# Attention block with an MLP: weight chunks loaded by halves, mask rows copied half as often, and small steps of the opening moved

## The reference

```python
q = _ln(queries, q_norm_g, q_norm_b); kv = _ln(tokens, kv_norm_g, kv_norm_b)
qp = q @ in_proj_w[:D].T + in_proj_b[:D]          # kp, vp from kv in the same way
scores = jnp.einsum('bhld,bhtd->bhlt', qh, kh) / np.sqrt(hd)
dist = jnp.sqrt(jnp.maximum(jnp.sum(diff * diff, axis=-1), 0.0))
scores = scores - spatial_scale * dist + spatial_offset
scores = jnp.where(key_padding, -jnp.inf, scores); attn = softmax(scores)
x = queries + (attn @ v) @ out_proj_w.T + out_proj_b
h = gelu(_ln(x, mlp_norm_g, mlp_norm_b) @ mlp_w1.T + mlp_b1)
x = x + (h @ mlp_w2.T + mlp_b2)
```

## Time and profile before

| | us |
|---|---|
| median of 3 runs | 1239.07 (1238.29 to 1239.6) |
| the profiled execution | 1240.29 |
| its span, first to last instruction | 1238.5 |
| PE busy | 1209.4 (98%) |
| POOL busy | 992.2 (80%) |
| DVE busy | 935.5 (76%) |
| ACT busy | 876.5 (71%) |

### The profile page before, as it was taken

How to read it: one execution, slowest core, us unless ns; L and a number is a source line. 1 busy time by engine, 2 the same in 40 slices (tenths; PEclk the granted TensorE clock), 3 DMA queues, 4 the chain that set the end, 5 groups by cost and what they waited for, 6 DMA issues and landing times.

```text
span 1238.5 us, 27536 instructions
## 1 busy us (share of the span) xinstructions
PE 1209.4 (98%) x9320; PEld 788.6 (64%) x9320; DVE 935.5 (76%) x2467; ACT 876.5 (71%) x2062; POOL 992.2 (80%) x1287
## 2 busy tenths in 40 slices
PE   7899899999999999999999999999999999999998
PEld 3444465666666666666666666667666666666664
DVE  5789998888877787888877787788777777677321
ACT  6889777777767776777767776777767776776331
POOL 5587999989897989989897989989898987767320
PEclk9999999999999999999999999999999999999999
DMA  8599998998998898999889998988989998888544
GB/s 240 156 204 224 251 233 183 209 209 178 208 195 212 194 224 179 213 206 184 202 192 217 196 221 183 214 201 188 203 192 209 197 216 171 168 177 176 143 113 125
DMA packets 469693, 241.69 MB, mean 195 GB/s; under 512 B 385056, under 2 KB 409904, under 8 KB 469552
## 3 DMA queue, kind: packets, MB, share of 16 engines
q1 hardware_dynamic: 469552, 239.93, 86.3%
HBM read 109.66 MB, written 12.58 MB: 99 GB/s over the span
## 4 chain that ended last, share of the span: by engine, by line
PE 85%; SPq 4%; POOL 3%; DVE 3%; issue 2%; ACT 2%; DMA 1%; POOLq 0%; DVEq 0%; ACTq 0%
PE ps_down L685 26%; PE ps_up L670 26%; PE ps_qk L605 12%; PE ps_vo L629 6%; PE ps_vo L626 6%; PE ps_s L641 4%; PE ps_pv L655 4%; SPq L401 1%; SPq L423 1%; POOL soft L1341 1%; SPq L392 1%; POOL p_nat L1333 1%; SPq L462 1%; DMA w_stage<-in_w_qkv 0%; SPq L376 0%
## 5 line engine op out<-in xcount | busy, mean ns | idle before, releaser
L670 PE MATMUL ps_up<-hT,w 128*128 128x256 f16 x3072 | 377.2, 273 | 2.0 <-ACT u L884 1.3
L685 PE MATMUL ps_down<-w,hid 128*128 128x512 f16 x1536 | 372.8, 379 | 0.5 <-DVE hid L1177 0.4
L670 PEld LDWEIGHTS ps_up<-hT,w 128*128 128x128 f16 x3072 | 300.2, 98 | 91.8 <-issue 2.4
L1333 POOL TENSOR_SCALAR p_nat<-soft,row_inv 128x256 f16<-128x256 f32 x480 | 296.1, 626 | 62.5 <-DVE row_inv L1135 60.5
L837 ACT ACTIVATE soft<-soft,neg_max 128x256 f32<-128x256 f32 x512 | 255.2, 500 | 124.1 <-DVE neg_max L1127 123.3
L1127 DVE CUSTOM_DVE_ANT_0 soft<-ps_s,soft,factor 128x256 f32<-128x256 f32 x512 | 225.6, 476 | 142.3 <-PE ps_s L641 142.1
L1145 DVE SCALAR_TENSOR_TENSOR p_nat<-soft,row_inv,p_nat 128x256 f16<-128x256 f32 x480 | 266.4, 594 | 2.1 <-POOL p_nat L1333 2.1
L1341 POOL TENSOR_SCALAR soft<-dist,scale_neg,offset 128x512 f32<-128x512 f32 x256 | 248.7, 971 | 14.1 <-DVE p_nat L1145 10.3
L884 ACT ACTIVATE u<-ps_up,bias,up_scale 128x256 f32<-128x256 f32 x256 | 142.2, 556 | 133.4 <-PE ps_up L670 133.4
L685 PEld LDWEIGHTS ps_down<-w,hid 128*128 128x128 f16 x1536 | 148.6, 97 | 132.0 <-DMA w<-x_scratch 1.1
L1349 POOL TENSOR_SCALAR hid<-u,hid_scale 128x1024 f16<-128x1024 f32 x64 | 81.3, 1271 | 102.7 <-ACT u L890 102.3
(11 more groups left out here) (135 smaller groups left out, 1568.2 us busy)
## 6 DMA issues: line engine op xcount, KB each, us to landing
w<-x_scratch SPq DMA_DIRECT2D x256, 256.0 KB, 3.1
stack<-qk_parts SPq DMA_DIRECT2D x256, 96.0 KB
raw<-in_ctx SPq DMA_DIRECT2D x32, 256.0 KB, 3.5
raw<-in_x SPq DMA_DIRECT2D x32, 256.0 KB, 3.1
c_stage<-in_w SPq DMA_DIRECT2D x32, 256.0 KB, 4.0
x<-in_x SPq DMA_DIRECT2D x32, 256.0 KB, 3.3
out<-x SPq DMA_DIRECT2D x32, 256.0 KB, 3.2
tok_rows<-in_tok_xy SPq DMA_DIRECT2D x16, 256.0 KB, 3.8
```

Source lines behind the costliest of these rows:

```text
L670: mm = e.matmul(ps_up[s % 2][:, 0:L], w_1_sb[:, wp, k, m * P:(m + 1) * P], hT[:, b % 2, :, xp * KT + k, :], start=(k, wp, xp) == (0, 0, 0) ...
L685: mm = e.matmul(ps_down[tt][:], hid[:, chunk % HID_RING, i, hp, tt * P:(tt + 1) * P], w_2_sb[:, s % W2_RING, wp, :], start=(m == 0 and (hp ...
L1333: mine = e.tensor_scalar(p_nat[:, nat, HI, lc, :], soft[:, ring, lc, :], row_inv[:, ring, lc:lc + 1], 1.0, ALU.mult, ALU.mult)
```

## The change

- W1 and W2 are loaded in 16 DMAs of 512 KB in place of 32 of 256 KB, one every second slot, each when both quarters that it overwrites have been split; each staging buffer has two semaphores instead of four.
- `stack_copies` copies the mask row only for the first two groups of a batch (each ring place once a batch), and `n_stack` counts accordingly.
- `row_q` gets its own place, so `dist_square` no longer waits for the DMA that reads it; `bias_rows_1` takes that wait over.
- `masks` moves from slot -5 to -24 (DVE), `keep_mask` from -4 to -18 (SP).
- `dist_sqrt(0)` moves from slot -4 to -6, ahead of the sum of V's squares (ACT). The squares of the first two quarters move from slots -4 and -3 to -2.
- The row of V: `weight_bias` from slot -3 to 0 (PE), `bias_row` from -2 to 1 (ACT), `bias_turn` from -1 to 2 (SP), `bias_v_spread` from 3 to 4 (DVE). `keep_busy` in slot 0 counts 16 steps more as taken (as slot 4 does), and `warm` in slot -6 has 8 matmuls instead of 6.

```diff
--- before.py
+++ after.py
@@ -153,7 +153,7 @@
         sq = sb("sq", [P, LC, T], F32, at["x1_n"])
 
         row_kv = sb("row_kv", [1, D], F32, at["x1"] + KT * D * 4)
-        row_q = sb("row_q", [1, D], F32, at["x1_n"])
+        row_q = sb("row_q", [1, D], F32, at["h_nat"] + 2 * D * 2)
         rows_1 = sb("rows_1", [P, D], F32, at["x1"] + (KT + 1) * D * 4)
         bias_v = sb("bias_v", [P, KT, P], F32, at["x1"] + KT * D * 4)
         mask_u8 = sb("mask_u8", [B, T], U8, at["x1"] + (KT + 1) * D * 4)
@@ -214,7 +214,7 @@
         s_m1, s_u, s_gelu, s_hidhi, s_hidlo, s_m2, s_out = [
             sem(n) for n in ("s_m1", "s_u", "s_gelu", "s_hidhi", "s_hidlo", "s_m2", "s_out")]
         s_w2, s_store = sems("s_w2_", W2_RING), sems("s_store", X1_RING)
-        s_w, s_wk, s_wq, s_wc = sems("s_w", 2), sems("s_wk", KT), sems("s_wq", KT), [sems(f"s_wc{i}_", KT) for i in range(C_STAGES)]
+        s_w, s_wk, s_wq, s_wc = sems("s_w", 2), sems("s_wk", KT), sems("s_wq", KT), [sems(f"s_wc{i}_", 2) for i in range(C_STAGES)]
         s_colsq, s_colsum, s_wsq, s_tot, s_mix, s_n2, s_pow, s_gs, s_cst = [
             sem(n) for n in ("s_colsq", "s_colsum", "s_wsq", "s_tot", "s_mix", "s_n2", "s_pow", "s_gs", "s_cst")]
         s_whi, s_wlo, s_w2st, s_invw, s_wh = sem("s_whi"), sem("s_wlo"), sems("s_w2st", W2_RING), sem("s_invw"), sem("s_wh")
@@ -263,7 +263,8 @@
             return 2 * G + which + 1
 
         def n_stack(G):
-            return 5 * DMA * (G // STACK_RING + 1)
+
+            return DMA * (HPG * (G // STACK_RING + 1) + G // HG + 1)
 
         def n_pt(i):
             return DMA * (i // PT_RING + 1)
@@ -352,11 +353,13 @@
             src = w_o if sec == SEC_O else w_qkv[:, sec * D:(sec + 1) * D]
             return src.rearrange("(k p) n -> p k n", p=P)
 
-        def c_src(n, k):
+        def c_half(n, half_of):
             if n < N_CHUNKS:
-                return w_1[k * P:(k + 1) * P, n * D:(n + 1) * D]
-            m = KT * (n - N_CHUNKS) + k
-            return w_2[m * P:(m + 1) * P, :]
+                rows = w_1[2 * half_of * P:(2 * half_of + 2) * P, n * D:(n + 1) * D]
+            else:
+                m = KT * (n - N_CHUNKS) + 2 * half_of
+                rows = w_2[m * P:(m + 2) * P, :]
+            return rows.rearrange("(k p) n -> p k n", p=P)
 
         def staged(n, k):
             return c_stage[n % C_STAGES][:, k, :]
@@ -390,8 +393,9 @@
                     src = qk_parts[32 * j:32 * j + 32, :, G % 2:G % 2 + 2, :].rearrange("p r w l -> p r (w l)")
                     dst = stack[0:96, ring, j, :, :].rearrange("p w l -> p (w l)")
                     e.dma_start(dst, src).then_inc(s_stack[ring], DMA)
-                src = mask_kept[b:b + 1, :].rearrange("p (o t) -> p o t", o=1).to_broadcast([1, HPG, T])
-                e.dma_start(stack[96:97, ring, :, 1 - query_side(G), :], src).then_inc(s_stack[ring], DMA)
+                if G % HG < STACK_RING:
+                    src = mask_kept[b:b + 1, :].rearrange("p (o t) -> p o t", o=1).to_broadcast([1, HPG, T])
+                    e.dma_start(stack[96:97, ring, :, 1 - query_side(G), :], src).then_inc(s_stack[ring], DMA)
 
             def p_turn(i):
                 gate.wait_ge(s_plo, i + 1)
@@ -454,12 +458,13 @@
                 for k in range(KT):
                     e.dma_start(w_stage[sec][:, k, :], w_src(sec)[:, k, :]).then_inc((s_wk if sec == SEC_K else s_wq)[k], DMA)
 
-            def load_chunk(n, k):
+            def load_chunk(n, half_of):
 
                 if n >= C_STAGES:
-                    gate.wait_ge(s_wlo, n_piece(n - C_STAGES, k))
+                    gate.wait_ge(s_wlo, n_piece(n - C_STAGES, 2 * half_of + 1))
                     gate.wait_ge(s_brow, 3 + min(n - C_STAGES + 1, N_CHUNKS))
-                e.dma_start(staged(n, k), c_src(n, k)).then_inc(s_wc[n % C_STAGES][k], DMA)
+                dst = c_stage[n % C_STAGES][:, 2 * half_of:2 * half_of + 2, :]
+                e.dma_start(dst, c_half(n, half_of)).then_inc(s_wc[n % C_STAGES][half_of], DMA)
 
             def store_w2(s):
                 gate.wait_ge(s_wlo, n_piece(N_CHUNKS, s))
@@ -496,12 +501,12 @@
                     load_out_bias()
                 if slot == 6:
                     load_mlp_bias()
-                for sec, at_slot in ((SEC_K, -25), (SEC_Q, -24), (SEC_V, -1)):
+                for sec, at_slot in ((SEC_K, -25), (SEC_Q, -24), (SEC_V, 2)):
                     if slot == at_slot:
                         bias_turn(sec)
                 if slot == 18:
                     bias_turn_1()
-                if slot == -4:
+                if slot == -18:
                     keep_mask()
                 for G in due(slot, QK_PROJ + 4, GROUP, N_HG):
                     stack_copies(G)
@@ -525,8 +530,8 @@
                         load_residual(2 * b + tt)
                     for b in due(slot, DOWN + MT + 2 + tt, BATCH, B):
                         store_out(2 * b + tt)
-                for step in due(slot, -6, ITEM, 2 * N_CHUNKS * KT):
-                    load_chunk(*divmod(step, KT))
+                for step in due(slot, -6, 2 * ITEM, 2 * N_CHUNKS * 2):
+                    load_chunk(*divmod(step, 2))
             for ring in range(X1_RING):
                 last = (N_TILES - 1 - ring) // X1_RING
                 e.wait_ge(s_store[ring], DMA * (last + 1))
@@ -551,7 +556,7 @@
 
             def w1_bias(c, k):
 
-                gate.wait_ge(s_wc[c % C_STAGES][k], n_staged(c))
+                gate.wait_ge(s_wc[c % C_STAGES][k // 2], n_staged(c))
                 mm = e.matmul(ps_bias_1[32 * c:32 * c + 1, :], cols_sb[:, B_M + k:B_M + k + 1], staged(c, k),
                               start=(k == 0), stop=(k == KT - 1))
                 if k == KT - 1:
@@ -709,14 +714,14 @@
             VO_FILL = 6
             qk, vo, vo_ready = qk_project(), vo_project(), 0
             for slot in range(FIRST_SLOT, LAST_SLOT + 1):
-                for at_slot, count in ((-32, 10), (-30, 1), (-28, 1), (-8, 12), (-6, 6)):
+                for at_slot, count in ((-32, 10), (-30, 1), (-28, 1), (-8, 12), (-6, 8)):
                     if slot == at_slot:
                         warm(count)
                 if slot == -32:
                     column_totals()
                 if -1 <= slot < UP:
                     scores(slot + 1)
-                for sec, at_slot in ((SEC_K, -31), (SEC_Q, -29), (SEC_V, -3)):
+                for sec, at_slot in ((SEC_K, -31), (SEC_Q, -29), (SEC_V, 0)):
                     if slot == at_slot:
                         weight_bias(sec)
                 if slot == 0:
@@ -748,7 +753,7 @@
                 if 0 <= slot < DOWN:
                     taken = 1 + (3 if due(slot, 9, GROUP, N_HG) else 0) + (6 if slot % 2 else 0) + (6 if slot >= UP else 0)
                     taken += vo_done + (4 if due(slot, 1, ITEM, MT) else 0)
-                    taken += 16 if slot == 4 else 0
+                    taken += 16 if slot in (0, 4) else 0
                     keep_busy(ps_pv if slot < 9 else ps_down[0], max(0, SLOT_STEPS - taken))
                 for s in due(slot, DOWN, ITEM, N_STEPS):
                     mlp_down(s)
@@ -775,7 +780,7 @@
                              accum_out=sums[:, of_tensor(w)]).then_inc(s_wsq)
 
             def chunk_square(n, k):
-                gate.wait_ge(s_wc[n % C_STAGES][k], n_staged(n))
+                gate.wait_ge(s_wc[n % C_STAGES][k // 2], n_staged(n))
                 gate.wait_ge(s_row, ROW_Q)
                 gate.wait_ge(s_wh, KT * n + k)
                 e.activation(ps_down[1][:], staged(n, k), ACT.Square, accum_out=ssq[:, KT * n + k:KT * n + k + 1]).then_inc(s_wh)
@@ -792,6 +797,7 @@
 
             def bias_rows_1():
                 gate.wait_ge(s_brow, 3 + N_CHUNKS)
+                gate.wait_ge(s_rowd[SEC_Q], DMA)
                 gate.wait_ge(s_mkept, DMA)
                 gate.wait_ge(s_colsum, 1)
                 e.activation(by_column(rows_1[0:97, :]), ps_bias_1[0:97, :].rearrange("p (m q) -> p m q", m=KT), ACT.Copy).then_inc(s_row)
@@ -863,7 +869,6 @@
                 gate.wait_ge(s_bias, H * (b - DIST_RING + 1))
                 gate.wait_ge(s_d2, b)
                 gate.wait_ge(s_hlo, 2 * (b - 2))
-                gate.wait_ge(s_rowd[SEC_Q], DMA)
                 for lc in range(LC):
                     dst = (dist[:, b % DIST_RING, lc, :], sq[:, lc, :])[c]
                     col = (b * LC + lc) * 2 + c
@@ -913,7 +918,7 @@
                 for tt in range(TC):
                     for b in due(slot, V_PROJ[tt] + 2, BATCH, B):
                         v_hi(b, tt)
-                for sec, at_slot in ((SEC_K, -26), (SEC_Q, -24), (SEC_V, -2)):
+                for sec, at_slot in ((SEC_K, -26), (SEC_Q, -24), (SEC_V, 1)):
                     if slot == at_slot:
                         bias_row(sec)
                 if slot == 17:
@@ -926,6 +931,8 @@
                 for sec, at_slot in ((SEC_K, -31), (SEC_Q, -30)):
                     if slot == at_slot:
```

(15 more changed lines are left out.)

## The result

The changed kernel takes 1242.97 us (median of 20 runs, 1239.38 to 1245.49), the kernel before 1239.34 (20 runs, 1237.28 to 1242.2): ratio 1.0028, 95% interval 1.0020 to 1.0036. It is slower, by 3.6 us, where 2.2 us less was forecast.

A forecast was written before the change was run, and what follows sets the result against it. PE, busy 98%, was taken as the bound, so only the opening to about 195 us could gain, with SP's queue binding 65 to 117; 0.2 + 1.6 + 0.4 = 2.2 us, median 1239.07 to 1236.9, range 1233.8 to 1240.2.

The forecast's parts named there:

- PE is ahead of that: Slots 0 to 2: PE's eight matmuls replace seven fillers and it stays ahead of ACT; score_max(4) 2.0 to 2.2 us earlier.
- Rival D: Spread late in slot 4, L565 at 60.4, b_o 2.1 us later, late halves another 0.7: 1241.9 us; chance 0.11.
- Slow clock: Opening: changed PE gaps may alter the granted clock; put at nothing, since ACT sets slots 0 and 1.
- Until slot 4: 0 to 58 us: earlier steps gain about 2 us, slot 4 takes it back; 0.2 us left, bounds -2.1 and +0.6.
- 65 to 117 us: SP's stretch: 4.2 us less on SP's queue, of which ACT's 1.6 us is gained; bounds 0 and 2.9.
- PE idle between 1 and 2: Sign that the forecast is right: PE's idle from 65 to 117 us falls to between 1 and 2 us.
- C: Nothing gets through: DVE, ACT, DMA take SP's place; gain 0 to 0.8 us, PE idle stays 2.9; chance 0.19 with E.
- 117 to 195 us: Four issues and two mask rows less, 3 us of SP; 0.4 us gained, bounds -0.5 and 2.
- The cost of an issue: 65 to 117 us: a 512 KB issue costs SP what 256 KB does, saving 3.4 us of its queue.
- E: A 512 KB load lands later, about 4.6 us; ACT waits 0.5 us in 16 slots, losing 1.6; 0.19 with C.

The follow-up runs named there:

- clock_fill: total_first_spread3 with more filler matmuls in three gaps ahead of slot 0 (slots -6, -3, -1): 1239.59 us, 0.9994 of before.
- early_no_squares: The kernel before with the early steps (row_q, masks, keep_mask, distance root, warm), the two squares left in place: 1240.66 us, 0.9999 of before.
- squares_only: The kernel before with the first two chunk squares alone moved to slot -2: 1241.57 us, 1.0013 of before.
- halves_only: The kernel before with the loads by halves alone: 1238.81 us, 0.9980 of before.
- halves_masks: The kernel before with the loads by halves and the mask rows copied half as often: 1237.95 us, 0.9979 of before.
- row_v_only: The kernel before with V's row alone moved, and the 16 steps in slot 0: 1243.49 us, 1.0031 of before.
- total_first: The changed kernel with O's total issued ahead of weight_bias(V) in slot 0: 1241.53 us, 1.0011 of before.
- row_v_back: The changed kernel with V's row alone put back, and no extra 16 steps in slot 0: 1239.97 us, 1.0004 of before.
- total_first_spread3: total_first with the spread back in slot 3 as well: 1238.49 us, 0.9994 of before.
- fill_before_l570: The changed kernel with nine filler matmuls in slot 4 ahead of value_bias_out: 1241.09 us, 1.0010 of before.
- loads_early_no_squares: The kernel before with all of the change but the squares' move and V's row: 1238.91 us, 0.9986 of before.

## Why the prediction was wrong, point by point

**The step that failed: "PE is ahead of that", in the stage until slot 4.** The prediction let `score_max(4)` come 2.0 to 2.2 us earlier, started L565 at 58.2 and took 0.2 us of gain from the stage. Found: `score_max(4)` 0.3 us earlier, the matmuls at 60.61, a loss of 2.3 at their start. The gain in slots 1 and 2 came from a sum over ACT and PE ("PE is ahead of that: slot 0 gets the eight matmuls (3.6 to 4.95) for the seven fillers, 2.8"). That sum counted what PE has to do in slot 0 and left out the order within the slot: O's total stands behind the eight matmuls, and DVE waits for it with `score_max(1)` behind (7.17 us for 1.97). The rows for that were in the trace of before (DVE waited 1.97 us for this total at 39.70). With O's total first and the spread back the loss was gone (0.9994).

**Rival D, weighed 0.11,** had what follows from such a delay: the spread late in slot 4, L565 at 60.4, its sign ("score_max(4) comes less than 2 us earlier"), 1241.9. It didn't have the cause, since it thought of a late statistic or a saturated ACT. That its time lies only 1.1 us from 1242.97 is in part luck: its 0.7 for halves that land late is not what the runs show (the loads gain 0.2%), and the clock in slot 4 and the squares, which it lacked, stand against that gain.

**Slow clock: "nothing".** Nothing that can be told ahead of slot 0 (clock_fill 0.9994), wrong from slot 0 on. For a clock that stays low through slot 0 the prediction had 4.95 us for the eight matmuls and PE still at `scores(2)` 1 us early; they took 4.71, and `scores(2)` stood at 46.52, 0.4 us late (1.3, counted from `bias_row(K)`), with no wait in front of it: PE itself was late with what stands ahead. In slot 4 the prediction priced the matmuls of `value_bias_out` at 3.60 us, whatever gap came in front of them; with the forecast idle of over 1 us and a late spread they took 5.40. No rival had this term.

**Until slot 4.** ACT's wait for row_q is gone: L875 starts at 17.01 without one. Q's projection was forecast 0.46 us earlier. Counted from `bias_row(K)` on it starts 12.65 to 13.12 us later in the five kernels that keep the wait (mean 12.87), 12.20 to 12.96 in the nine without it (mean 12.40): 0.47 us, in the mean; in after itself, with 12.96, there is nothing of it. The number is right by luck, for both its terms were off. w_q's low parts were to begin 0.46 us earlier and take 3.24 us either way; counted from `bias_row(K)` they began as late as before (mean 9.02 us in the nine, 8.98 in the five), and took 2.73 in place of 3.24, without waits for ACT's high parts in them. They began no earlier because the masks, put at nothing, cost DVE time: 0.74 and 0.67 us instead of 0.27 and 0.28, and the next low part of x took 1.75 instead of 0.69, alike in all nine kernels that move the masks.

```profile
19.07 0.74 DVE L1092 TENSOR_SCALAR mask_f<-mask_u 16x256 f32<-16x256 uint8 x1
19.85 0.67 DVE L1094 TENSOR_SCALAR mask_row<-mask_f 16x256 f16<-16x256 f32 x1
20.45 1.75 DVE L1113 TENSOR_TENSOR x_nat<-raw,x_nat 128x512 f16<-128x512 f32 x1
```

Why they take longer there, and what the masks in their old place would have given, no run shows. In the median the early steps without the squares are worth nothing (early_no_squares 0.9999). K's second projection was at 29.85 (forecast 30.0), the stack copies at 29.82 (30.0), w_v at 31.64 (31.45). The copies took 3.39 us for four issues, 2.59 before, so `scores(0)` came only 0.9 us earlier, and no earlier at all counted from `bias_row(K)` (22.53 and 22.50):

```profile
29.82 3.39 SPq L395 DMA_DIRECT2D stack<-qk_parts  x4
```

```profile
35.40 0.60 PE L646 MATMUL ps_s<-stack 97*128 97x256 f16 x2 [2.81 <-DMA stack<-stack]
```

The squares were rightly counted as one more before the exponentials (behind w_v ACT does four in place of three until `exps(0)`), but their 0.65 was set against gains that didn't come, and ended as nothing in the sum. squares_only shows 0.13%, 1.6 us.

**65 to 117 us: 1.6.** Not found in this stretch, though the view the prediction asked for, "PE idle between 1 and 2", seems to say it is right: 1.8. PE came 4.1 us late and so had less to wait for. In halves_only, which is not late, the idle is 2.9 as before, which was the sign for C. SP has waits of its own, and POOL's wait for the transposes fell from 4.0 us to

```profile
POOL x_nat L1318 <- DMA xT<-x_nat: 0.9, 1, 0.9
```

but behind it DVE and ACT are the next late, as C said (48.20 and 49.16 of 52 us busy in halves_only).

**117 to 195 us: 0.4.** Near what the profiles show, 0.5 us (halves_only's lead grows from 2.7 us at 87 to 3.2 at 188).

**The cost of an issue, and E.** 512 KB cost SP what 256 KB did (median 460 ns, 438 before) and land in 4.9 us, 4.0 before; E expected 4.6. In after ACT waited for one of them for 0.7 us between 118 and 195 us. The page's row of these loads:

```profile
c_stage<-in_w SPq DMA_DIRECT2D x16, 512.0 KB, 4.9
```

E's mechanism is there once, not 16 times. The mask rows behind 195 us were rated at nothing, and all of them together are worth nothing that can be told (halves_only beside halves_masks).

**The range.** 1233.8 to 1240.2 left D out, whose time lay 1.7 us above it. D's sum was 2.8 us and the loss is 3.6. The runs' own balance is another one than D's: V's row 3.8 us (0.31%, with some 1.8 of clock in it), the early steps 2.4 (0.19%, the squares 1.6 of them), and the loads a gain of 2.6 (0.21%), none of which D had in this way. The forecast gain of 1.6 + 0.4 us for SP's relief is about what the loads alone give; where it arises is another place than forecast, and open.

## What to carry to other kernels

When an instruction is moved into a slot of an in-order engine, look at what stands behind it in the same slot and who waits for that; a small total behind eight fp32 matmuls held DVE for 7.17 us instead of 1.97. Mind an idle gap in front of expensive matmuls: price them at both clock levels (3.60 and 5.40 us), and try to fill the gap if the input can't come earlier. Read a smaller idle time behind a late arrival as what it is, and give several changes at once their own runs: here one part gained 0.2%, and two others hid it. Ask whether the one profile that you read is a typical run before you take a clock from it.

## What the runs showed of the hardware

In after, gaps of 1.15 and 2.06 us in front of 54.94 and 60.61 were followed by granted clock 0.50, and in row_v_only gaps of 1.15 and 2.04; in total_first gaps of 1.71 and 1.16, in front of 53.70 and 58.47, were not. So two such gaps don't always bring it down. The slow stretch also moves: in the six kernels with V's row put back, moved alone, or mended (row_v_back, row_v_only, total_first, total_first_spread3, fill_before_l570, clock_fill) the profile has one or two at clock 0.50 between 134 and 197 us, which the other eight profiles don't have; whether they belong to the kernels or to the runs is open. In the opening, 42 to 44 us ran at 0.50 to 0.58 in before, early_no_squares and halves_masks, and at 1.00 in halves_only and loads_early_no_squares:

```profile
42.00:44.00 2.00, 2.00 (x14) 1.12 (x12) 0.65 (x6) 2.00 (x9) 1.20 (x2) 1.00 0.87 281
```

(halves_only) beside

```profile
42.00:44.00 2.00, 2.00 (x7) 0.73 (x6) 1.67 (x10) 1.99 (x7) 0.18 (x1) 0.58 0.74 232
```

(before). Over the three groups' runs of before a mean clock lower by 0.001 goes with 0.6 to 0.9 us more (slope of a straight line). By that, as an estimate, after's 0.9920 against 0.9955 in the first group's before would be 2.2 to 3.1 of its 3.6 us; but total_first_spread3, at 0.9933, is no slower than before, so a low clock alone does not tell a slow kernel. Nor does the opening start alike: the first 13 us differ by up to 1.1 us between the profiles, before any instruction that the kernels don't share.
